# A language-model tower on one core: where the elementwise work of the gate, the last norm and the quantisations is done

## The reference

```
h = take(embed, x)
h = h + L0_attn(layernorm(h))     # in-projection, causal conv, silu, cumulative sum, gate, out-projection
h = h + L0_ffn(layernorm(h))      # norm; 154 routed tokens per sequence go through softmax attention
                                  # (12 heads of 16), the others through a mixing product; then a gelu MLP
h = h + L1_attn(layernorm(h))
h = h + L1_ffn(layernorm(h))

# L1_attn: a from softmax attention of 12 heads, a1 from attention on 100 memory slots
alpha = sigmoid(concat([a, a1]) @ w_alpha + b_alpha)
fused = alpha * a + (1 - alpha) * a1
return fused @ w_proj + b_proj

# L1_ffn: twice a bit-linear layer with a gelu between
xn = x * rsqrt(mean(x * x) + eps) * g
scale = 127 / clip(max(abs(xn)), 1e-5)
xq = clip(round(xn * scale), -128, 127) / scale
y = xq @ weight_quant(w)
```

## Time and profile before

| | |
|---|---|
| median of 3 runs | 2289.93 us (2288.05 to 2291.09) |
| the profiled execution, its own time | 2290.06 us |
| its span, first to last instruction | 2288.3 us |
| PE busy | 1812.2 us (79%) |
| DVE busy | 1454.4 us (64%) |
| ACT busy | 982.0 us (43%) |
| POOL busy | 119.8 us (5%) |

### The profile page before, as it was taken

One profiled execution on the slowest core, in us unless ns is written; L12 is line 12 of the kernel. 1 busy time (PEld: TensorE's weight loads), 2 busy tenths in 40 slices (PEclk: granted clock), 3 DMA queues, 4 the chain that ended last, 5 costly groups with the idle time before them and its releaser, 6 DMA issues.

```text
span 2288.3 us, 27535 instructions
## 1 busy us (share of the span) xinstructions
PE 1812.2 (79%) x9834; PEld 957.4 (42%) x9834; DVE 1454.4 (64%) x3296; ACT 982.0 (43%) x1371; POOL 119.8 (5%) x163
## 2 busy tenths in 40 slices
PE   1786778998999899984566787899889898998735
PEld 1365447662333233353244554756423322333613
DVE  4747774047777677747667767522577767774786
ACT  0331331234666466641532234121466655667143
POOL 4010000000000000004011000000000000000010
PEclk9977785997999799996577778789889998999856
DMA  5011110012000010000000111000300100000000
GB/s 127 0 45 31 43 29 0 1 51 67 22 22 22 18 25 22 8 1 25 4 28 1 56 43 46 2 1 0 111 15 23 25 23 15 22 21 1 1 0 28
DMA packets 57644, 58.48 MB, mean 26 GB/s; under 512 B 27063, under 2 KB 35556, under 8 KB 57510
## 3 DMA queue, kind: packets, MB, share of 16 engines
q1 hardware_dynamic: 55894, 53.57, 9.2%
q0 software_dynamic: 1616, 3.16, 0.6%
HBM read 38.51 MB, written 18.16 MB: 25 GB/s over the span
## 4 chain that ended last, share of the span: by engine, by line
PE 57%; DVE 35%; issue 3%; ACT 3%; SPq 1%; DMA 1%; POOL 0%; DVEq 0%; ACTq 0%
DVE nmp L1419 9%; PE PV L803 8%; PE S L760 7%; PE ST L784 6%; PE ST L530 4%; PE ST L718 4%; DVE nmp L1351 3%; PE S L755 2%; PE MT L810 2%; DVE Er L1447 2%; PE S L615 2%; PE PV L643 2%; DVE st L1254 2%; PE S L729 2%; DVE R L1467 1%
## 5 line engine op out<-in xcount | busy, mean ns | idle before, releaser
L1419 DVE TENSOR_REDUCE nmp<-S 128x1 f32<-128x512 f32 x768 | 493.3, 686 | 120.5 <-PE S L760 116.4
L1087 ACT ACTIVATE Er<-ST 128x1024 f32<-128x1024 f32 x384 | 391.5, 1024 | 254.3 <-PE ST L784 246.7
L760 PE MATMUL S<-KS,QS 96*128 96x512 bf16 x768 | 316.1, 417 | 66.0 <-DVE nmp L1419 40.9
L784 PE MATMUL ST<-QS,KS 100*128 100x512 bf16 x768 | 238.7, 393 | 5.1 <-ACT QS L1078 3.6
L760 PEld LDWEIGHTS S<-KS,QS 96*128 96x128 bf16 x768 | 75.1, 98 | 327.2 <-DVE nmp L1419 243.0
L803 PE MATMUL PV<-Er,V 128*17 128x512 f32 x1536 | 205.4, 607 | 0.0
L1351 DVE TENSOR_REDUCE nmp<-S 80x1 f32<-80x512 f32 x192 | 120.7, 679 | 29.1 <-PE S L615 26.2
L615 PE MATMUL S<-KS,QS 96*80 96x512 bf16 x192 | 88.5, 498 | 32.3 <-DVE nmp L1351 22.2
L430 POOL TENSOR_SCALAR tp<-mv 128x8 f32<-128x8 f32 x20 | 5.1, 257 | 1998.7 <-DVE mv L1258 1998.7
L784 PEld LDWEIGHTS ST<-QS,KS 100*128 100x128 bf16 x768 | 68.8, 100 | 93.1 <-issue 48.7
L1407 DVE TENSOR_REDUCE junk<-S 128x68 f32<-128x272 f32 x96 | 42.4, 442 | 101.0 <-PE S L755 101.0
(11 more groups left out here) (363 smaller groups left out, 3173.5 us busy)
## 6 DMA issues: line engine op xcount, KB each, us to landing
KS<-scr_k SPq DMA_DIRECT2D x576, 32.0 KB, 1.8
scr_k<-R SPq DMA_DIRECT2D x16, 576.0 KB, 4.0
QS<-scr_q SPq DMA_DIRECT2D x288, 32.0 KB, 1.8
scr_q<-R SPq DMA_DIRECT2D x8, 576.0 KB, 4.9
out_dram<-HS SPq DMA_DIRECT2D x8, 384.0 KB, 2.8
QS<-scr_q SPq DMA_DIRECT2D x48, 30.0 KB, 1.9
wf<-in_L_ffn_W_dram SPq DMA_DIRECT2D x2, 576.0 KB
scr_q<-small SPq DMA_DIRECT2D x8, 90.0 KB, 2.0
```

What stands on the lines that cost most here:

```text
L760: ins = nc.tensor.matmul(S[n % 2][:, :], QS[0:KP, h % KRING, (u // 2) * P:(u // 2 + 1) * P], KS[0:KP, h % KRING, (u % 2) * HALF:(u % 2 + 1 ...
L784: ins = nc.tensor.matmul(ST[i % 2][:, (kt % 2) * HALF:(kt % 2 + 1) * HALF], KS[0:KP + 4, h % KRING, kt * P:(kt + 1) * P], queries, start=T ...
L1087: A_(E[:, g, :], ST[i % 2][:, :], ACT.Exp).then_inc(s["exps"], 1)
L1419: v.tensor_reduce(nmp[:, u // 2, u % 2:u % 2 + 1], S[n % 2][:, :], AX.X, ALU.max).then_inc(s["reduced"], 1)
```

## The change

Five edits:

1. ACT takes Sigmoid of the gate's product instead of exp(-x). GpSimd computes the difference `DIF = U - X` into a free part of `R`. DVE's `fuse` is left with the product and the sum.
2. ACT does the last norm as Identity with scale 1/deviation and bias -mean/deviation, 8 instructions for a slot. GpSimd computes the bias `nb` with two more small instructions. DVE's `quantise` begins with the gain.
3. The second step of the first quantisation (768 elements for each half of a slot) is done by GpSimd.
4. So is the second step of the hidden quantisation, one instruction of 768 elements for a tile.
5. The gather writes into the buffer of `V`, seen as `G`. It is issued for the second pair after the values' last use and after `DIF` of both slots. The column of ones is set again after each residual; the two memsets of `V` at the start go.

```diff
+            o.G = o.V[:, :, :, :].rearrange("p t h d -> p (t h d)")[:, 0:T * D].rearrange("p (t d) -> p t d", t=T)
+            o.DIF = R[:, 2 * L:2 * L + T * D].rearrange("p (t d) -> p t d", t=T)
...
+        def DONE(p, o):
+            return at(p, o, NUNITS, NUNITS + 2)
+        def PVS(p, o):
+            return at(p, o, NSTEP, NSTEP + RING)
@@ GpSimd, inverse_deviation
-                g.tensor_tensor(o.rnn[:], o.rnn[:], o.rn[:], ALU.mult).then_inc(o.s["rstd"], 1)
+                ins = g.tensor_tensor(o.rnn[:], o.rnn[:], o.rn[:], ALU.mult)
+                if n == 4:
+                    link(ins)
+                    link(g.tensor_tensor(o.nb[:], o.mv[:, :, 0], o.rnn[:], ALU.mult))
+                    ins = g.tensor_scalar(o.nb[:], o.nb[:], -1.0, None, ALU.mult)
+                ins.then_inc(o.s["rstd"], 1)
@@ GpSimd, the queue of a pair
-                for n in range(5):
+                for n in range(4):
                     for o in slots:
-                        inverse_deviation(p, o, n, {1: LN_EPS, 4: RMS_EPS}.get(n))
+                        inverse_deviation(p, o, n, LN_EPS if n == 1 else None)
+                for o in slots:
+                    g.wait_ge(s["reduced"], DONE(p, o))
+                    g.tensor_tensor(o.DIF[:, :, :], o.U[:], o.X[:], ALU.subtract).then_inc(s["dif"], 1)
                 if p + 1 < NPAIR:
                     for o in slots:
-                        g.wait_ge(o.s["evac"], p * 28 + 30)
+                        g.wait_ge(s["pv"], PVS(p, o))
                         gather(p + 1, o)
+                for o in slots:
+                    inverse_deviation(p, o, 4, RMS_EPS)
+                for o in slots:
+                    for half in range(2):
+                        g.wait_ge(s["qmul"], at(p, o, 2, half + 1))
+                        g.tensor_scalar(o.XQ[:, HT * half:HT * half + HT, :], o.X[:, HT * half:HT * half + HT, :], MAGIC, None, ALU.subtract).then_inc(s["quant"], HT)
                 for half in range(2):
...
+                    for t in range(HT * half, HT * half + HT):
+                        for o in slots:
+                            g.wait_ge(o.s["hmul"], p * 8 + t + 1)
+                            if t >= 2:
+                                g.wait_ge(o.s["hturned"], p * 8 + t - 1)
+                            g.tensor_scalar(o.HQ[:, (t % 2) * F:(t % 2 + 1) * F], o.HG[:, t % HT, :], MAGIC, None, ALU.subtract).then_inc(o.s["hquant"], 1)
@@ ScalarE
-                        A_(o.e2[...], o.D2[i % 2][...], ACT.Exp, scale=-1.0).then_inc(s["alphae"], 1)
+                        A_(o.e2[...], o.D2[i % 2][...], ACT.Sigmoid).then_inc(s["alphae"], 1)
                 for o in slots:
                     evac(p, o, 6, o.XT)
+                for o in slots:
+                    act.wait_ge(o.s["rstd"], p * 5 + 5)
+                    for t in range(T):
+                        ins = A_(o.X[:, t, :], o.HS[:, t, :], ACT.Identity, scale=o.rnn[:, t:t + 1], bias=o.nb[:, t:t + 1])
+                    ins.then_inc(s["ln4"], 1)
@@ VectorE, fuse
+                ve.wait_ge(s["dif"], at(p, o, 1, 1))
                 for i in range(4):
                     ve.wait_ge(s["alphae"], at(p, o, 4, i + 1))
-                    v.tensor_scalar(e, e, 1.0, None, ALU.add)
-                    link(v.tensor_tensor(own, own, mem, ALU.subtract))
-                    link(v.reciprocal(e, e))
-                    link(v.tensor_tensor(own, own, e, ALU.mult))
-                    v.tensor_tensor(own, own, mem, ALU.add).then_inc(s["fusedx"], 1)
+                    e, d = o.e2[:, i % 2, :, :], o.DIF[:, 2 * i:2 * i + 2, :]
+                    link(v.tensor_tensor(d, d, e, ALU.mult))
+                    v.tensor_tensor(o.U[:, 2 * i:2 * i + 2, :], d, o.X[:, 2 * i:2 * i + 2, :], ALU.add).then_inc(s["fusedx"], 1)
@@ VectorE, quantise
-                ve.wait_ge(o.s["rstd"], p * 5 + 5)
-                for t in range(T):
-                    ins = v.tensor_scalar(o.X[:, t, :], o.HS[:, t, :], o.mv[:, t, 0:1], o.rnn[:, t:t + 1], ALU.subtract, ALU.mult)
-                link(ins)
+                ve.wait_ge(s["ln4"], at(p, o, 1, 1))
...
-                    link(v.tensor_scalar(o.X[:, t, :], o.X[:, t, :], o.qsc[:, t:t + 1], MAGIC, ALU.mult, ALU.add))
-                    v.tensor_scalar(o.XQ[:, t, :], o.X[:, t, :], MAGIC, None, ALU.subtract).then_inc(s["quant"], 1)
+                    ins = v.tensor_scalar(o.X[:, t, :], o.X[:, t, :], o.qsc[:, t:t + 1], MAGIC, ALU.mult, ALU.add)
+                    if t % HT == HT - 1:
+                        ins.then_inc(s["qmul"], 1)
@@ VectorE, quantise_hidden
-                link(v.tensor_scalar(o.HG[:, t % HT, :], o.HG[:, t % HT, :], o.qsc[:, t:t + 1], MAGIC, ALU.mult, ALU.add))
-                if t >= 2:
-                    ve.wait_ge(o.s["hturned"], p * 8 + t - 1)
-                v.tensor_scalar(o.HQ[:, (t % 2) * F:(t % 2 + 1) * F], o.HG[:, t % HT, :], MAGIC, None, ALU.subtract).then_inc(o.s["hquant"], 1)
+                v.tensor_scalar(o.HG[:, t % HT, :], o.HG[:, t % HT, :], o.qsc[:, t:t + 1], MAGIC, ALU.mult, ALU.add).then_inc(o.s["hmul"], 1)
@@ VectorE, the start, and behind the residual of each slot
-                link(v.memset(o.V[:], 0.0))
-                link(v.memset(o.V[:, :, :, DH:DH + 1], 1.0))
...
+                    v.memset(o.V[:, :, :, DH:DH + 1], 1.0)
```

More of the change, by code:

```diff
@@ L162, in build @@
         OWN = """gathered stats rstd xnorm turned evac inproj inproj_out conv silu gated proj hi resid mid lo vproj vcopied
-            hidden gelu ffn h2 bhid bgelu hss hrms hquant hturned hcopied bout outs stored kw0 kw1 qw0 qw1""".split()
+            hidden gelu ffn h2 bhid bgelu hss hrms hmul hquant hturned hcopied bout outs stored kw0 kw1 qw0 qw1""".split()
         slots = []
@@ L210, in build @@
             o.rnn = sb("rnn" + nx, [P, T])
+            o.nb = sb("nb" + nx, [P, T])
             o.tp = sb("tp" + nx, [P, T])
@@ L248, in build @@
             units0 reduced0 units reduced rowmax mturned mcopied acc0 ctxr accout st0 ex0 pv0 ctxn ctxt ctxtc att atts
-            pooled mixin mixed merged stile exps pv alpha alphae fusedx fproj h3 quant qturned qcopied
+            pooled mixin mixed merged stile exps pv dif alpha alphae fusedx fproj h3 ln4 qmul quant qturned qcopied
             vlink plink filled pp pa pd kr0 kr1 kr2 kr3 qr0 qr1 qr2 qr3 q0w q0r mw mr""".split()
@@ L448, in gather @@
                     b = 2 * p + o.x
-                    g.indirect_dma_start(o.U[:, t, :], None, A["L0_tok_embed_matrix"][:],
+                    g.indirect_dma_start(o.G[:, t, :], None, A["L0_tok_embed_matrix"][:],
                                          bass.IndirectOffsetOnAxis(ap=tok_i[:, b * T + t:b * T + t + 1], axis=0)).then_inc(o.s["gathered"], 16)
@@ L1172, in _ @@
                             act.wait_ge(s["fusedx"], at(p, o, 4, i - 1))
-                        A_(o.e2[:, i % 2, :, :], o.D2[i % 2][:, 0:2 * D].rearrange("p (t d) -> p t d", t=2), ACT.Exp, scale=-1.0).then_inc(s["alphae"], 1)
+                        A_(o.e2[:, i % 2, :, :], o.D2[i % 2][:, 0:2 * D].rearrange("p (t d) -> p t d", t=2), ACT.Sigmoid).then_inc(s["alphae"], 1)
                 for o in slots:
                     evac(p, o, 6, o.XT)
+                for o in slots:
[3 more added lines that the diff above has]
+                    ins.then_inc(s["ln4"], 1)
                 for o in slots:
@@ L1494, in _ @@
                     ve.wait_ge(o.s["gathered"], p * 128 + 128)
-                    stats(p, o, o.U)
+                    stats(p, o, o.G)
                 for o in slots:
-                    normalise(p, o, 0, o.U, o.rn)
+                    normalise(p, o, 0, o.G, o.rn)
                 for c in range(2):
@@ L1506, in _ @@
                         ve.wait_ge(s["outproj"], at(p, o, 4, i + 1))
-                        v.tensor_tensor(o.HS[:, 2 * i:2 * i + 2, :], o.D2[i % 2][:, 0:2 * D].rearrange("p (t d) -> p t d", t=2), o.U[:, 2 * i:2 * i + 2, :], ALU.add).then_inc(s["h1"], 1)
+                        v.tensor_tensor(o.HS[:, 2 * i:2 * i + 2, :], o.D2[i % 2][:, 0:2 * D].rearrange("p (t d) -> p t d", t=2), o.G[:, 2 * i:2 * i + 2, :], ALU.add).then_inc(s["h1"], 1)
                     ve.wait_ge(s["h1"], at(p, o, 4, 4))
+                    v.memset(o.V[:, :, :, DH:DH + 1], 1.0)
                     stats(p, o, o.HS)
```

2 lines of the change are left out of this document (removed).

## The result

The changed kernel takes 2297.84 us (median of 7 runs, 2296.88 to 2300.76); the kernel before took 2289.93 in the same comparison (7 runs, 2287.32 to 2291.7). The ratio is 1.0037, interval 1.0025 to 1.0049: slower by 0.4%. The forecast was 2263 with a range of 2250 to 2278; the time lies outside it, on the side of the third rival.

What follows compares the result with a forecast made beforehand. DVE was taken to bound each pair's tail: gate, last norm with first quantisation, hidden quantisation. Gate -34.0, norm and first quantisation -2.4 and -4.2, second steps +12.8, memsets +0.6 sum to -27.2 us: 2290.06 to 2263, range 2250 to 2278.

Steps and rivals of the forecast that it cites:

- the third rival: Second steps on GpSimd: a pass takes 1.8 us or more, decisive from 1.7; 2301 us at 2.0; chance 0.04.
- The pass on GpSimd: Second quantisation steps: one GpSimd pass of 768 elements takes 0.9 us, bounds 0.56 and 1.6.
- The hidden part: Hidden quantisation with its second step on GpSimd: +0.7 us a round, +6.4 us a pair.
- Blocking: Hidden quantisation: DVE's multiplies hold the shared ports, so GpSimd's pass waits; a round takes 3.06 us against 2.36.
- The gate: After the second slot's attention: PE no longer waits for DVE, so the first residual add comes 17.0 us earlier a pair.
- the fourth rival: Gate: smaller gain, as the table load is on the path or turns wait for ACT; 3 us a pair, 2269; chance 0.09.
- Norm and first quantisation: Last norm on ACT, first quantisation's second step on GpSimd: 2.4 us saved a pair, 4.2 in the first with the gathers.
- The gathers: Moved from behind the last norm into GpSimd's idle time after the second attention: 1.8 us saved, once.

Runs made afterwards that it cites:

- the fast form: The changed kernel with GpSimd's two second steps written as times 1, add -MAGIC instead of subtract MAGIC: 2270.78 us, ratio 0.9907 against the changed kernel.

## Why the prediction was wrong

**The pass on GpSimd: the step that failed.** "By the cast's slope it takes 0.18+0.73 = 0.9 us", with 1.6 as the upper bound. Measured 2.12 free and 2.28 in the mean. The slope of the cast was read rightly; that a subtraction goes at a cast's pace was the error, and the upper bound came from the same row. The hidden part cost +20.6 and +20.4 us a pair and not +6.4. This is the third rival, to which I gave 0.04: it decides from 1.7 us a pass, and gave 2301 at 2.0. Its formula gives 16 x 2.12 - 8.8 = 25.1 us a pair, 4.6 more than measured. Most of that is the full blocking in it: for the last four tiles GpSimd starts 0.71 us after DVE's first multiply does and not 2.25. The Trainium skill (GPSIMD Engine Reference, Elementwise — side-by-side cycle accounting) gives 1.03 cycles an element where the port limits and 1.8 as the best of a tight loop. At its 1.2 GHz the trace has 1.0 cycles for multiply-add (0.83 ns), as the page has it, and 3.0 for one operation (2.47 ns), for which neither figure holds.

**Blocking.** Assumed: GpSimd waits for both of DVE's multiplies, 0.54 us more a round. It doesn't: in both forms it starts 0.1 us behind the first, and its pass is 0.3 us longer (1.13 against 0.83, 2.44 against 2.12); the 2.74 us of the last four tiles are 0.62 longer. Wrong in mechanism, small in size: with the fast form the hidden part costs about 2.3 us a pair.

**The gate.** 17.0 forecast; 16.9 and 16.8 measured, table load hidden, PE without its pause, the low clock gone. Right, mechanism and size; the fourth rival is out.

**Norm and first quantisation.** -2.4 forecast for the second pair and -4.2 for the first. From DVE's end of the residual's statistics to the first hidden tile the traces have -1.1 and -2.9. ACT's norm was right (3.61 against 3.5); the 1.3 us are again the pass, 2.2 us here (with the fast form that stretch is another 2.0 us shorter, 23.5 against 25.5). With the second step left on DVE the norm gives 1.9 to 3.1 us a pair (tails of 118.6 with gate and gathers alone, 115.5 and 116.7 with the norm on ACT). Moving the first quantisation's second step costs 1 to 2 us a pair in the slow form (117.5 and 117.7), and in the fast form nothing that shows in the tails (115.7 and 116.5): the stretch to the first hidden tile is 0.8 us shorter, and the part behind it 0.6 to 0.9 longer.

**The gathers.** Costed as a gain of 1.8 us. The gain is there (tail1 120.2 with the gate alone, 118.6 with the gathers moved). What I did not see is that work beside which they now lie can stop for 9 to 12 us; the changed kernel happened not to, so this is no part of the miss, but it takes 9 to 12 us in six of the twelve kernels profiled with all gathers at the gate.

**The sum, with both put right.** 2262.9 less 2 x 4.1 for a hidden part of +2.3 and not +6.4 is 2254.7; the three kernels with the fast form, all gathers at the gate and no hole took 2255.7, 2256.5 and 2258.1, one execution each.

## What to carry to other kernels

A slope is a price for the operation it was read from: a cast's row prices a cast. Before a step moves to GpSimd, measure its very form, here operation 0, operation 1 and all, at the size it will have; a bound taken from the same row as the estimate is no bound. And a stage that goes from one engine to another on the path, with no overlap to win, needs the new engine to be about as fast: here 16 passes a pair, each 1.56 us longer (2.12 against 0.56), cost 20.5 of the 25 us that this adds up to. An engine that takes on work in the middle of the path also holds it up with whatever stands ahead in its queue, here eight gathers.

## What was not expected of the hardware

- GpSimd's tensor_scalar from f32 to bf16 or f32, 768 elements: 2.12 to 2.16 us for a subtract, an add or a multiply with constants (2.20 for a multiply with a column's value), 2.79 for subtract-multiply and subtract-add, 0.83 for multiply-add with constants and 0.91 with a column's value and a constant.
- Where DVE's one-input tensor_scalar and GpSimd's meet, both get longer: 0.83 to 1.13 us for GpSimd's pass, 0.61 to 1.19 for DVE's multiply; neither waits for the whole instruction of the other.
- With 16 indirect gathers in flight ACT can stand still 4.5 and 8.7 us with its input ready, and goes on 1.4 us after the last gather's packet starts. It did so in six of twelve kernels; what decides it is open.
